# Graph layer with residual norm on one core: the last output computed by whole rows and late halves, and PSUM copies moved ahead in the first steps

## The chip, the cores and the metric

The kernel runs on one core of one Trainium2 chip. The metric is the device time of one execution in microseconds (us). The engines are named as the profile names them: PE is TensorE, DVE is VectorE, ACT is ScalarE, POOL is GpSimd, SP is the engine that issues the DMAs. Each has its own instruction queue, kept in order; they meet at semaphores only.

## What is computed

For 32 batches of x (256 x 512) and an adjacency matrix adj (256 x 256), all in float32:

```
v = x @ weight ; q = x @ wq ; k = x @ wk
alpha = max(q @ k^T, 0) * (adj != 0)
alpha = softmax(alpha, axis=1)            # over the first index n, per batch
y = x + alpha @ v
out = (y - mean(y)) / sqrt(var(y) + 1e-5) # over the 512 columns
```

## The kernel before

Two batches make a pair; there are 16 pairs, and a pair's output is four "rows" (tiles of 128 rows by 512 columns; rows 0 and 1 are the first batch, 2 and 3 the second). Every float32 operand is split into a high and a low part (`..._hi`, made by ACT, and `..._lo`, the rest, made by DVE or POOL), and each product is three matrix products, hi*hi, hi*lo, lo*hi (`add_chunk`, lines 320 to 322).

`wq @ wk^T` is folded once into one matrix g, so that a pair needs T = g*x^T, the scores S = x*T, V = x*w and the output O = P*V, with P the softmax. T and V are built by a Strassen-like scheme of seven products, P1 to P7, of 256 x 256 blocks A11, A12, A21, A22 and sums of blocks S1 to S4. P1, P6, P5, P3 accumulate in one PSUM tile `chain`, in that order, half by half (c = 0, 1). After P1, P6 and P5 ACT copies each half to the SBUF tile `parts` before the next product may be added to it: the PE waits for `t_copied` (for T) or `v_copied` (for V). P7 and P4 use `bank_y`, P2 `bank_z`; DVE adds those into `parts` (`sum_t`, line 1037; `sum_v`, line 1044), and P4 may not overwrite `bank_y` until `sum_t` has read P7 out of it (`t_summed`).

The order of each engine's work is written out by hand. The first steps (pair 0 and the second half of T for pair 1) stand apart, a loop over groups of two pairs follows, and the last pair has code of its own. In the first steps three lists matter here:

- ACT copies chain for T of pair 1 (`copy_second_t`, line 706) and, among those copies, makes the high parts of the softmax of pair 0, `split_p(0, r)` (line 771). Later come the four exponents of pair 1 (`exponent`, line 763) and the copies of chain for V of pair 1 (`copy_v`, line 711).
- DVE has, in this order, `split_p(0, 0)`, a sum, `split_p(0, 1)` to `split_p(0, 3)` (the low parts p_lo, line 1098, each after ACT's high part), `sum_t(0, A22, 0)` and `sum_t(0, A22, 1)`, then the low parts of T (line 1025) and the residual adds (line 1108). The PE's P4 halves each wait for one of those sums.
- POOL makes the block sums S3, S1, S2, S4 of pair 2 (line 1432) as soon as their input has landed.

The last pair ends with `fill_last_o`: eight halves of rows (128 x 256) on eight PSUM places, in the order rows 0, 1 (column half 0), rows 2, 3 (half 1), rows 0, 1 (half 1), rows 2, 3 (half 0). DVE adds x to each half as it comes. Rows 0 and 1 get their mean from accumulated sums and their variance from ACT's squares; rows 2 and 3 get both from DVE's bn_stats and bn_aggr. POOL raises the variances to the power -1/2, two rows at a time. ACT scales row 0, DVE rows 1, 3, 2, and SP stores each row (256 KB) as it is done, in the order 0, 1, 3, 2.

Of the kernel before, what the change touches and what calls it, by code (L numbers as in the profile page):

```python
# [5 lines left out]
ALU = mybir.AluOpType  # L6
# [5 lines left out]
P = 128  # L12
EPS = 1e-5
# [22 lines left out]
A11, A12, A21, A22 = range(4)  # L36
# [24 lines left out]
def gnn_resnorm(nc: bass.Bass, x, x_t, adj_t, w, wq_t, wk_t, out):  # L61
# [14 lines left out]
    with ExitStack() as ctx:  # L76
        def sb(name, shape, dt=F32):
            return ctx.enter_context(nc.sbuf_tensor(name, shape, dt))
# [48 lines left out]
        rstd_a = sb("rstd_a", [P, R])  # L127
        shift = sb("shift", [P, R])

        half_sum = sb("half_sum", [P, M, 2])  # L130
        half_stats = sb("half_stats", [P, M, 2, 6])
        row_stats = sb("row_stats", [P, M, 2])

# [23 lines left out]
        def w_sum(b):  # L157
# [50 lines left out]

        LAST_HALVES = [(A11, 0, 0), (A11, 1, 0), (A22, 2, 1), (A22, 3, 1),
                       (A12, 0, 1), (A12, 1, 1), (A21, 2, 0), (A21, 3, 0)]
        last_to = [o_bank[0][:, 0], o_bank[1][:, 0], o_bank[2][:, 1], bank_y[:, 0, 1],
                   bank_z[:, 1], chain[:, 0, 1], chain[:, 1, 0], bank_y[:, 1, 0]]

# [5 lines left out]
        def _(sp):  # L221
# [81 lines left out]
            for t in range(2):  # L303
                sp.wait_ge(scaled, M * t + M)
                sp.dma_start(out_rows[PAIRS - 2][:, M * t:M * t + M],
                             xn[:, 0, M * t:M * t + M]).then_inc(y_stored[0], 16)
            for k, r in enumerate((0, 1, 3, 2)):
                if r == 0:
                    sp.wait_ge(scaled, R + 1)
                else:  # L310
                    sp.wait_ge(normed, R * (PAIRS - 2) + k)
                sp.dma_start(out_rows[PAIRS - 1][:, r], xn[:, 1, r]).then_inc(y_stored[1], 16)
# [5 lines left out]
        def _(pe):  # L318
# [303 lines left out]
            def fill_last_o():  # L622

                p = PAIRS - 1

                pe.wait_ge(added, R * p)
                for (u, r, j), to in zip(LAST_HALVES, last_to):
                    g, rows = u // 2, slice(r % M * P, (r % M + 1) * P)
                    if r % M == 0:
                        pe.wait_ge(p_lo_ready, R * p + M * g + M)  # L630
                        pe.wait_ge(v_lo_ready, R * p + V_LAST[u])
                    for m in range(M):
                        t = g * M + m
# [39 lines left out]
        def _(act):  # L673
# [313 lines left out]
            split_p(0, 0, first=True)  # L987
            split_p(0, 1)
            copy_second_t(P6)
            split_p(0, 2)  # L990
            split_p(0, 3)
            copy_second_t(P5)

            act.wait_ge(s_filled, 2)
            split_second_t(A11)
# [27 lines left out]
        def _(dve):  # L1023
# [324 lines left out]
            def add_half(n):  # L1348

                _, r, j = LAST_HALVES[n]  # L1350
                half = xn[:, 1, r, j * N:(j + 1) * N]
                dve.wait_ge(half_filled, n + 1)
                if r < M:
                    nc.vector.scalar_tensor_tensor(out=half, in0=last_to[n], scalar=1.0, in1=half, op0=ALU.mult,
                                                   op1=ALU.add, accum_out=half_sum[:, r, j:j + 1]).then_inc(half_added, 1)
                else:
                    nc.vector.tensor_tensor(half, last_to[n], half, ALU.add).then_inc(half_added, 1)

            def measure_half(n, after):
                _, r, j = LAST_HALVES[n]  # L1360
                dve.wait_ge(half_added, after)
                nc.vector.bn_stats(half_stats[:, r - M, j], xn[:, 1, r, j * N:(j + 1) * N]).then_inc(half_measured, 1)

            def measure_row(r, after):
                dve.wait_ge(half_measured, after)
                nc.vector.bn_aggr(row_stats[:, r - M], half_stats[:, r - M]).then_inc(row_measured, 1)

            def mean_of(r, after):
                dve.wait_ge(half_added, after)
                nc.vector.tensor_scalar(neg_mean[:, r:r + 1], half_sum[:, r, 0:1], half_sum[:, r, 1:2], -1.0 / D,  # L1370
                                        ALU.add, ALU.mult).then_inc(mean_ready, 1)

            def normalise_last(r):

                dve.wait_ge(rstd_ready, last + (0 if r < M else 1))
                if r < M:
                    nc.vector.tensor_scalar(xn[:, 1, r], xn[:, 1, r], neg_mean[:, r:r + 1], rstd[:, r:r + 1],
                                            ALU.add, ALU.mult).then_inc(normed, 1)
                else:
                    nc.vector.tensor_scalar(xn[:, 1, r], xn[:, 1, r], row_stats[:, r - M, 0:1], rstd[:, r:r + 1],  # L1380
                                            ALU.subtract, ALU.mult).then_inc(normed, 1)

            split_p(last, 0)
            split_p(last, 1)
# [15 lines left out]
            measure_half(2, 4)  # L1400
            add_half(4)
            mean_of(0, 5)
            add_half(5)
            mean_of(1, 6)
            measure_half(3, 6)
            add_half(6)
            measure_half(6, 7)
            measure_row(2, 3)
            add_half(7)
            dve.wait_ge(squared, R * last + M)  # L1410
            nc.vector.tensor_scalar(var_eps[:, 0:M], square_sum[:, 0:M], 1.0 / D, EPS, ALU.mult, ALU.add).then_inc(var_ready, 1)
            measure_half(7, 8)
            measure_row(3, 4)
            dve.wait_ge(row_measured, M)
            nc.vector.tensor_scalar(var_eps[:, M:R], row_stats[:, :, 1], EPS, None, ALU.add).then_inc(var_ready, 1)
            normalise_last(1)
            normalise_last(3)
            normalise_last(2)

        @block.gpsimd  # L1420
        def _(pool):
# [128 lines left out]
```

## Time and profile before

| quantity | value |
|---|---|
| time, median of 3 runs | 524.33 us (523.89 to 525.05) |
| profiled execution: its time / its span | 523.82 us / 522.0 us |
| PE busy | 511.8 us, 98% of the span |
| DVE, ACT, POOL busy | 368.1 (71%), 325.8 (62%), 258.1 us (49%) |
| mean granted PE clock | 0.995 of full speed |
| DMA | 62.05 MB, mean 119 GB/s |

The span runs from the first to the last instruction of the profile; the 1.8 us that the execution takes beyond it lie outside. Busy shares are means over the span. The PE's matrix products are pipelined: a 256-column product is listed as 0.28 us long, but the next one starts 0.12 us later, and only the distance of starts tells how fast the PE goes. After a wait of the PE the first product is listed as 0.38 or 0.39 us.

### The profile page before, as it was taken

What the parts mean: (1) busy time and instruction counts of PE and PEld (TensorE: products, weight loads), DVE (VectorE), ACT (ScalarE), POOL (GpSimd) and SP (SyncE); (2) the same over time, 40 slices, a digit from 0 to 9 for tenths busy, and PEclk for the clock granted to TensorE, in tenths of its full rate; (3) what the DMA queues carried; (4) which work ended last, traced back from release to release, by engine and by line L of the source; (5) the groups of instructions that cost most, each with busy time, mean ns of one, the idle gap of its engine ahead of it and who ended that gap; (6) DMA issues with size and microseconds to landing.
All of it is one profiled execution on the core that took longest, in us unless ns stands there. A gap on an engine that the chain in (4) does not pass through costs nothing.

```text
span 522.0 us, 9934 instructions
## 1 busy us (share of the span) xinstructions
PE 511.8 (98%) x3259; PEld 466.2 (89%) x3259; DVE 368.1 (71%) x746; ACT 325.8 (62%) x747; POOL 258.1 (49%) x196
## 2 busy tenths in 40 slices
PE   8999999999999999999999999999999999999994
PEld 5889998899989998899988999889998999889994
DVE  4766846776948677586866778577684867757686
ACT  5566556476763857539574586638676385764583
POOL 0397875239635386155661486433962537710011
PEclk9999999999999999999999999999999999999998
DMA  7404241044430626025350333404351061502334
GB/s 261 182 0 161 90 155 62 21 125 152 154 115 20 213 69 241 20 52 189 109 206 21 127 138 118 166 20 161 120 200 61 20 221 60 201 1 69 133 130 192
DMA packets 30735, 62.05 MB, mean 119 GB/s; under 512 B 2048, under 2 KB 3072, under 8 KB 30720
## 3 DMA queue, kind: packets, MB, share of 16 engines
q1 hardware_dynamic: 30720, 61.87, 34.2%
q8 instruction: 7, 0.11, 0.1%
q14 instruction: 8, 0.07, 0.0%
HBM read 45.09 MB, written 16.78 MB: 119 GB/s over the span
## 4 chain that ended last, share of the span: by engine, by line
PE 94%; DVE 2%; ACT 1%; DMA 1%; issue 0%; POOLq 0%; POOL 0%; SPq 0%; DVEq 0%; ACTq 0%
PE o_bank L320 12%; PE o_bank L321 12%; PE o_bank L322 12%; PE chain L320 11%; PE chain L322 11%; PE chain L321 11%; PE bank_y L320 6%; PE bank_y L321 6%; PE bank_y L322 6%; PE bank_z L320 3%; PE bank_z L321 3%; PE bank_z L322 3%; DMA xn<-in_w 1%; PE chain L502 0%; PE chain L503 0%; ACT v_hi L755 0%
## 5 line engine op out<-in xcount | busy, mean ns | idle before, releaser
L1441 POOL TENSOR_TENSOR s_lo<-xs,s_hi 128x512 fp32r<-128x512 f32 x60 | 82.6, 1394 | 33.9 <-ACT s_hi L692 33.9
L1436 POOL TENSOR_TENSOR a_lo<-xt,a_hi 128x512 fp32r<-128x512 f32 x42 | 57.9, 1386 | 61.2 <-ACT a_hi L684 61.2
L322 PE MATMUL o_bank<-t_hi,a_lo 128*128 128x256 f32 x256 | 72.4, 283 | 0.0
L321 PE MATMUL o_bank<-t_lo,a_hi 128*128 128x256 f32 x256 | 72.4, 283 | 0.0
L320 PE MATMUL o_bank<-t_hi,a_hi 128*128 128x256 f32 x256 | 72.4, 283 | 0.0
L1432 POOL TENSOR_TENSOR xs<-xt 128x512 f32<-128x512 f32 x30 | 40.0, 1347 | 47.8 <-DMA xt<-in_x_t 30.1
L1446 POOL TENSOR_TENSOR rstd<-var_eps,minus_half 128x4 f32<-128x4 f32 x14 | 14.2, 1018 | 92.6 <-DVE var_eps L1122 92.6
L711 ACT COPY parts<-chain 128x256 f32<-128x256 f32 x90 | 33.2, 370 | 39.5 <-PE chain L322 38.4
L320 PE MATMUL chain<-w_hi,s_hi 128*128 128x256 f32 x180 | 51.0, 284 | 0.5 <-ACT parts L711 0.5
L322 PE MATMUL chain<-w_hi,s_lo 128*128 128x256 f32 x180 | 50.9, 283 | 0.0
L321 PE MATMUL chain<-w_lo,s_hi 128*128 128x256 f32 x180 | 50.9, 283 | 0.0
L321 PEld LDWEIGHTS o_bank<-t_lo,a_hi 128*128 128x128 f32 x256 | 49.1, 192 | 0.3
L320 PEld LDWEIGHTS o_bank<-t_hi,a_hi 128*128 128x128 f32 x256 | 49.1, 192 | 0.3
L322 PEld LDWEIGHTS o_bank<-t_hi,a_lo 128*128 128x128 f32 x256 | 49.1, 192 | 0.0
L320 PE MATMUL o_bank<-v_hi,p_hi 128*128 128x512 f32 (+1 forms) x126 | 48.5, 385 | 0.0
L321 PE MATMUL o_bank<-v_lo,p_hi 128*128 128x512 f32 (+1 forms) x126 | 48.5, 385 | 0.0
L1037 DVE TENSOR_TENSOR parts<-parts,bank_y 128x512 f32<-128x512 f32 (+1 forms) x32 | 20.7, 653 | 39.2 <-ACT parts L701 25.8
L322 PE MATMUL o_bank<-v_hi,p_lo 128*128 128x512 f32 (+1 forms) x126 | 48.4, 384 | 0.0
L1025 DVE TENSOR_TENSOR v_lo<-parts,v_hi 128x512 fp32r<-128x512 f32 x45 | 47.6, 1071 | 0.9 <-ACT v_hi L755 0.9
L1108 DVE SCALAR_TENSOR_TENSOR xn<-o_bank,xn 128x512 f32<-128x512 f32 x60 | 40.9, 683 | 8.4 <-PE o_bank L322 8.4
L701 ACT COPY parts<-chain 128x512 f32<-128x512 f32 x42 | 24.7, 588 | 34.6 <-PE chain L322 34.1
L783 ACT ACTIVATE c_b<-xn,neg_mean 128x512 f32<-128x512 f32 x58 | 41.9, 722 | 3.4 <-DVE neg_mean L1370 2.4
(222 smaller groups left out, 1628.9 us busy)
## 6 DMA issues: line engine op xcount, KB each, us to landing
xt<-in_x_t SPq DMA_DIRECT2D x64, 256.0 KB, 3.2
xn<-in_x SPq DMA_DIRECT2D x16, 1024.0 KB, 5.2
out<-xn SPq DMA_DIRECT2D x14, 1024.0 KB, 5.4
adj<-in_adj_t SPq DMA_DIRECT2D x16, 512.0 KB, 6.0
xn<-in_w SPq DMA_DIRECT2D x4, 256.0 KB, 4.9
xn<-in_wq_t SPq DMA_DIRECT2D x4, 256.0 KB, 5.8
parts<-in_wk_t SPq DMA_DIRECT2D x4, 256.0 KB, 5.8
out<-xn SPq DMA_DIRECT2D x2, 512.0 KB, 2.8
```

The source lines that it names most:

```text
L320: nc.tensor.matmul(dst, a[0], b[0], start=first, stop=False, skip_group_check=shared)
L321: nc.tensor.matmul(dst, a[0], b[1], start=False, stop=False, skip_group_check=shared)
L322: return nc.tensor.matmul(dst, a[1], b[0], start=False, stop=last, skip_group_check=shared)
L701: nc.scalar.copy(parts[:, PART[product], c], chain[:, c]).then_inc(t_copied, 1)
L711: nc.scalar.copy(parts[:, PART[product], c, 0], chain_v[:, c]).then_inc(v_copied, 1)
L783: nc.scalar.activation(squares, xn[:, slot, r], ACT.Square, bias=neg_mean[:, r:r + 1], accum_out=square_sum[:, r:r + 1]).then_inc(squared, 1)
L1025: return nc.vector.tensor_tensor(dst, whole, hi.bitcast(F32), ALU.subtract)
L1037: nc.vector.tensor_tensor(part, part, bank, ALU.add).then_inc(t_summed, 1)
L1108: nc.vector.scalar_tensor_tensor(out=xn[:, slot, r], in0=row.rearrange("q j n -> q (j n)"), scalar=1.0, in1=xn[:, slot, r], op0=ALU.mult, ...
L1432: nc.gpsimd.tensor_tensor(xs[:, s], a, b, op).then_inc(x_summed[slot], 1)
L1436: nc.gpsimd.tensor_tensor(a_lo[:, slot, u], xt[:, u], a_hi[:, slot, u].bitcast(F32), ALU.subtract).then_inc(a_lo_ready[slot], 1)
L1441: nc.gpsimd.tensor_tensor(s_lo[:, slot, s], xs[:, s], s_hi[:, slot, s].bitcast(F32), ALU.subtract).then_inc(s_lo_ready[slot], 1)
```

## The change

It has two parts. In the first steps ACT's list is reordered: the two copies of P5 go ahead of `split_p(0, 2)` and `split_p(0, 3)`, and the two copies of P1 for V of pair 1 go between the exponents of pair 1. At the end, rows 0 and 1 of the last output are computed whole and first, on `o_bank[0]` and `o_bank[1]`, and only rows 2 and 3 by halves; DVE uses `residual` and a mean by row, rows 2 and 3 get a variance and a power each, and they are scaled and stored in the order 2, 3.

```diff
-        LAST_HALVES = [(A11, 0, 0), (A11, 1, 0), (A22, 2, 1), (A22, 3, 1),
-                       (A12, 0, 1), (A12, 1, 1), (A21, 2, 0), (A21, 3, 0)]
+        LAST_HALVES = [(A22, 2, 1), (A22, 3, 1), (A21, 2, 0), (A21, 3, 0)]
+        last_to = [o_bank[2][:, 1], bank_y[:, 0, 1], chain[:, 0, 0], chain[:, 1, 0]]
...
-            for k, r in enumerate((0, 1, 3, 2)):
+            for k, r in enumerate((0, 1, 2, 3)):
...
                 pe.wait_ge(added, R * p)
+                pe.wait_ge(p_lo_ready, R * p + M)
+                pe.wait_ge(v_lo_ready, R * p + V_LAST[A12])
+                for r in range(M):
+                    fill_row(r, o_bank[r][:])
+                pe.wait_ge(p_lo_ready, R * p + R)
...
             copy_second_t(P6)
+            copy_second_t(P5)
             split_p(0, 2)
             split_p(0, 3)
-            copy_second_t(P5)
...
-            for r in range(R):
-                exponent(1, r)
+            exponent(1, 0)
+            exponent(1, 1)
             copy_v(1, P1, 0)
+            exponent(1, 2)
             copy_v(1, P1, 1)
+            exponent(1, 3)
...
+            def variance_of(r):
+                dve.wait_ge(row_measured, r - M + 1)
+                nc.vector.tensor_scalar(var_eps[:, r:r + 1], row_stats[:, r - M, 1:2], EPS, None, ALU.add).then_inc(var_ready, 1)
...
             sum_v(last, A21)
+            residual(last, GROUPS - 1, 1, 0)
+            mean_of(0)
             split_v(last, A21, V_LAST)
-            dve.wait_ge(xn_loaded[1], 16 * GROUPS)
-            for n in range(R):
-                add_half(n)
+            residual(last, GROUPS - 1, 1, 1)
+            mean_of(1)
...
-            for t in range(2):
-                rows = slice(M * t, M * t + M)
-                pool.wait_ge(var_ready, PAIRS + t)
+            for k, rows in enumerate((slice(0, M), slice(M, M + 1), slice(M + 1, R))):
+                pool.wait_ge(var_ready, PAIRS + k)
                 nc.gpsimd.tensor_tensor(rstd[:, rows], var_eps[:, rows], minus_half[:, rows],
                                         ALU.pow).then_inc(rstd_ready, 1)
```

What follows is how the instructions stand, engine by engine (line numbers of each kernel's own source; in the changed kernel they are shifted by 1 to 3).

ACT in the first step, before: L706 are the copies of chain, first those of P1, then P6, then P5; L771 are the high softmax parts of rows 0, 1, then 2, 3; L745 are the high parts of T.

```order
L706 COPY parts<-chain 128x256 x2
L771 ACTIVATE p_hi<-soft,inv_sum 128x256 x2
L706 COPY parts<-chain 128x256 x2
L771 ACTIVATE p_hi<-soft,inv_sum 128x256 x2
L706 COPY parts<-chain 128x256 x2
L745 CAST t_hi<-parts 128x512 x2
```

And in the changed kernel:

```order
L707 COPY parts<-chain 128x256 x2
L772 ACTIVATE p_hi<-soft,inv_sum 128x256 x2
L707 COPY parts<-chain 128x256 x4
L772 ACTIVATE p_hi<-soft,inv_sum 128x256 x2
L746 CAST t_hi<-parts 128x512 x2
```

The two copies of P5 moved ahead of the softmax parts of rows 2 and 3; nothing else did.

ACT in the second step, before: L763 are the four exponents of pair 1, L711 the copies of chain for V (P1, P6, P5, two halves each).

```order
L692 CAST s_hi<-xs 128x512 x4
L763 ACTIVATE soft,exp_sum<-soft,neg_max 128x256 x4
L711 COPY parts<-chain 128x256 x6
L684 CAST a_hi<-xt 128x512
L692 CAST s_hi<-xs 128x512
```

And in the changed kernel:

```order
L693 CAST s_hi<-xs 128x512 x4
L764 ACTIVATE soft,exp_sum<-soft,neg_max 128x256 x2
L712 COPY parts<-chain 128x256
L764 ACTIVATE soft,exp_sum<-soft,neg_max 128x256
L712 COPY parts<-chain 128x256
L764 ACTIVATE soft,exp_sum<-soft,neg_max 128x256
L712 COPY parts<-chain 128x256 x4
```

The two copies of P1 moved ahead of the third and the fourth exponent.

DVE at the end of the program, before, from the last low part of V on:

```order
L1025 TENSOR_TENSOR v_lo<-parts,v_hi 128x2x256
L1354 SCALAR_TENSOR_TENSOR xn,half_sum<-o_bank,xn 128x256 x2
L1357 TENSOR_TENSOR xn<-o_bank,xn 128x256
L1357 TENSOR_TENSOR xn<-bank_y,xn 128x256
L1362 BN_STATS half_stats<-xn 128x6
L1354 SCALAR_TENSOR_TENSOR xn,half_sum<-bank_z,xn 128x256
L1370 TENSOR_SCALAR neg_mean<-half_sum 128x1
L1354 SCALAR_TENSOR_TENSOR xn,half_sum<-chain,xn 128x256
L1370 TENSOR_SCALAR neg_mean<-half_sum 128x1
L1362 BN_STATS half_stats<-xn 128x6
L1357 TENSOR_TENSOR xn<-chain,xn 128x256
```

And in the changed kernel, from the first residual row on:

```order
L1111 SCALAR_TENSOR_TENSOR xn,y_sum<-o_bank,xn 128x512
L1370 TENSOR_SCALAR neg_mean<-y_sum 128x1
L1028 TENSOR_TENSOR v_lo<-parts,v_hi 128x2x256
L1111 SCALAR_TENSOR_TENSOR xn,y_sum<-o_bank,xn 128x512
L1370 TENSOR_SCALAR neg_mean<-y_sum 128x1
L1356 TENSOR_TENSOR xn<-o_bank,xn 128x256
L1361 BN_STATS half_stats<-xn 128x6
L1356 TENSOR_TENSOR xn<-bank_y,xn 128x256
L1398 TENSOR_SCALAR var_eps<-square_sum 128x2
L1361 BN_STATS half_stats<-xn 128x6
L1356 TENSOR_TENSOR xn<-chain,xn 128x256
```

Two whole rows with their means stand where four halves with accumulated sums stood, one of them ahead of the last low part of V, and the variance of rows 0 and 1 comes five instructions earlier in the measuring of rows 2 and 3.

## Rows read from the trace of the kernel before

**Rows 1.** Chain of waits, whole span, by engine: share of the span.
```profile
PE 94%; DVE 2%; ACT 1%; DMA 1%; issue 0%; POOLq 0%; POOL 0%; SPq 0%; DVEq 0%; ACTq 0%
```

**Rows 2.** Timeline, PE, 52 to 54.1 us: start, duration, engine, line, operation, output<-inputs, shapes.
```profile
52.10 0.28 PE L322 MATMUL chain<-s_hi,g_lo 128*128 128x256 f32 x1
52.48 0.38 PE L320 MATMUL chain<-s_hi,g_hi 128*128 128x256 f32 x1
...
54.01 0.28 PE L320 MATMUL bank_y<-a_hi,g_hi 128*128 128x256 f32 x1
```

**Rows 3.** Timeline, ACT, 50.9 to 52.8 us.
```profile
50.98 0.37 ACT L706 COPY parts<-chain 128x256 f32<-128x256 f32 x1 [0.34 <-PE chain L322]
51.25 0.91 ACT L771 ACTIVATE p_hi<-soft,inv_sum 128x256 fp32r<-128x256 f32 x2
52.06 0.73 ACT L706 COPY parts<-chain 128x256 f32<-128x256 f32 x2
```

**Rows 4.** Timeline, DVE, 51.8 to 53.4 us; in brackets idle before, and its end.
```profile
51.80 0.88 DVE L1098 SCALAR_TENSOR_TENSOR p_lo<-soft,inv_sum,p_hi 128x256 fp32r<-128x256 f32 x2 [1.36 <-ACT p_hi L771]
52.60 0.74 DVE L1037 TENSOR_TENSOR parts<-parts,bank_y 128x256 f32<-128x256 f32 x2
```

**Rows 5.** Timeline, POOL, 53 to 54.5 us.
```profile
53.23 1.30 POOL L1432 TENSOR_TENSOR xs<-xt 128x512 f32<-128x512 f32 x1 [4.28 <-DMA xt<-in_x_t]
```

**Rows 6.** Timeline, DVE and POOL, about 83.8 and about 117.5 us.
```profile
83.03 1.30 POOL L1441 TENSOR_TENSOR s_lo<-xs,s_hi 128x512 fp32r<-128x512 f32 x1 [1.62 <-ACT s_hi L692]
83.81 0.80 DVE L1098 SCALAR_TENSOR_TENSOR p_lo<-soft,inv_sum,p_hi 128x256 fp32r<-128x256 f32 x1
...
117.46 0.48 DVE L1098 SCALAR_TENSOR_TENSOR p_lo<-soft,inv_sum,p_hi 128x256 fp32r<-128x256 f32 x1
117.59 1.50 POOL L1436 TENSOR_TENSOR a_lo<-xt,a_hi 128x512 fp32r<-128x512 f32 x1 [8.55 <-ACT a_hi L684]
```

**Rows 7.** Timeline, PE, at 69.5 us: the start of P6 in the second step.
```profile
69.53 0.39 PE L320 MATMUL chain<-w_hi,s_hi 128*128 128x256 f32 x1 [0.54 <-ACT parts L711]
```

**Rows 8.** Timeline, ACT, 68.1 to 69.8 us.
```profile
68.13 0.51 ACT L763 ACTIVATE soft<-soft,neg_max 128x256 f32<-128x256 f32 x1 [1.75 <-DVE soft L1087]
...
69.13 0.62 ACT L711 COPY parts<-chain 128x256 f32<-128x256 f32 x2
```

**Rows 9.** Timeline, PE: first 512-column product of a pair, and what follows the 24.
```profile
493.48 0.40 PE L320 MATMUL o_bank<-v_hi,p_hi 128*128 128x512 f32 x1
...
498.95 0.28 PE L320 MATMUL chain<-w_hi,a_hi 128*128 128x256 f32 x1
```

**Rows 10.** Timeline, DVE, the end of the program and two rows like the new ones.
```profile
499.04 0.68 DVE L1108 SCALAR_TENSOR_TENSOR xn<-o_bank,xn 128x512 f32<-128x512 f32 x1
...
499.84 0.54 DVE L1128 TENSOR_SCALAR xn<-xn,neg_mean,rstd 128x512 f32<-128x512 f32 x1
...
508.57 0.68 DVE L1025 TENSOR_TENSOR v_lo<-chain,v_hi 128x512 fp32r<-128x512 f32 x1
...
512.74 0.43 DVE L1362 BATCH_NORM_STATS2 half_stats<-xn 128x6 f32<-128x256 f32 x1
...
514.59 0.41 DVE L1357 TENSOR_TENSOR xn<-chain,xn 128x256 f32<-128x256 f32 x1
...
516.88 0.57 DVE L1377 TENSOR_SCALAR xn<-xn,neg_mean,rstd 128x512 f32<-128x512 f32 x1
517.71 1.00 DVE L1380 TENSOR_SCALAR xn<-xn,row_stats,rstd 128x512 f32<-128x512 f32 x2 [0.26 <-POOL rstd L1521]
```

**Rows 11.** Timeline, POOL, after 516 us.
```profile
516.14 1.53 POOL L1521 TENSOR_TENSOR rstd<-var_eps,minus_half 128x2 f32<-128x2 f32 x2 [10.83 <-DVE var_eps L1411]
```

**Rows 12.** Timeline, SP's DMA issues, after 517 us.
```profile
517.62 1.82 SPq L312 DMA_DIRECT2D out<-xn  x4
```

**Rows 13.** Stretches at the end: length, busy time by engine, granted clock, DMA share, GB/s.
```profile
518.50:521.00 2.50, 0.00 (x0) 0.00 (x0) 0.21 (x1) 0.00 (x0) 0.00 (x0) 0.50 1.05 406
521.00:521.50 0.50, 0.00 (x0) 0.00 (x0) 0.00 (x0) 0.00 (x0) 0.00 (x0) 0.50 0.13 45
```

More of the change, by code:

```diff
@@ L128, in gnn_resnorm @@
         shift = sb("shift", [P, R])
-        half_sum = sb("half_sum", [P, M, 2])
         half_stats = sb("half_stats", [P, M, 2, 6])
@@ L207, in gnn_resnorm @@
             sem("half_added"), sem("half_measured"), sem("row_measured"), sem("centred"))
-        LAST_HALVES = [(A11, 0, 0), (A11, 1, 0), (A22, 2, 1), (A22, 3, 1),
-                       (A12, 0, 1), (A12, 1, 1), (A21, 2, 0), (A21, 3, 0)]
-        last_to = [o_bank[0][:, 0], o_bank[1][:, 0], o_bank[2][:, 1], bank_y[:, 0, 1],
-                   bank_z[:, 1], chain[:, 0, 1], chain[:, 1, 0], bank_y[:, 1, 0]]
+        LAST_HALVES = [(A22, 2, 1), (A22, 3, 1), (A21, 2, 0), (A21, 3, 0)]
+        last_to = [o_bank[2][:, 1], bank_y[:, 0, 1], chain[:, 0, 0], chain[:, 1, 0]]
         block = ctx.enter_context(nc.Block())
@@ L626, in fill_last_o @@
                 pe.wait_ge(added, R * p)
+                pe.wait_ge(p_lo_ready, R * p + M)
[3 more added lines that the diff above has]
+                pe.wait_ge(p_lo_ready, R * p + R)
                 for (u, r, j), to in zip(LAST_HALVES, last_to):
-                    g, rows = u // 2, slice(r % M * P, (r % M + 1) * P)
-                    if r % M == 0:
-                        pe.wait_ge(p_lo_ready, R * p + M * g + M)
+                    rows = slice(r % M * P, (r % M + 1) * P)
+                    if r == M:
                         pe.wait_ge(v_lo_ready, R * p + V_LAST[u])
                     for m in range(M):
-                        t = g * M + m
+                        t = M + m
                         last = add_chunk(to, (p_hi[:, t, rows], p_lo[:, t, rows]), (v_hi[:, t, j], v_lo[:, t, j]),
@@ L1352, in add_half @@
                 dve.wait_ge(half_filled, n + 1)
[L1353 to L1359, printed above, removed]
+                nc.vector.tensor_tensor(half, last_to[n], half, ALU.add).then_inc(half_added, 1)
@@ L1360, in measure_half, with measure_row @@
+            def measure_half(n):
                 _, r, j = LAST_HALVES[n]
-                dve.wait_ge(half_added, after)
+                dve.wait_ge(half_added, n + 1)
                 nc.vector.bn_stats(half_stats[:, r - M, j], xn[:, 1, r, j * N:(j + 1) * N]).then_inc(half_measured, 1)
-            def measure_row(r, after):
-                dve.wait_ge(half_measured, after)
+            def measure_row(r):
+                dve.wait_ge(half_measured, r + 1)
                 nc.vector.bn_aggr(row_stats[:, r - M], half_stats[:, r - M]).then_inc(row_measured, 1)
[L1368 to L1381, printed above, removed]
+            def mean_of(r):
+                dve.wait_ge(added, R * last + r + 1)
+                nc.vector.tensor_scalar_mul(neg_mean[:, r:r + 1], y_sum[:, r:r + 1], -1.0 / D).then_inc(mean_ready, 1)
@@ L1395, in _ @@
             sum_v(last, A21)
+            residual(last, GROUPS - 1, 1, 0)
+            mean_of(0)
             split_v(last, A21, V_LAST)
-            dve.wait_ge(xn_loaded[1], 16 * GROUPS)
-            for n in range(R):
-                add_half(n)
[L1400 to L1409, printed above, removed]
+            residual(last, GROUPS - 1, 1, 1)
+            mean_of(1)
+            add_half(0)
+            measure_half(0)
+            add_half(1)
             dve.wait_ge(squared, R * last + M)
             nc.vector.tensor_scalar(var_eps[:, 0:M], square_sum[:, 0:M], 1.0 / D, EPS, ALU.mult, ALU.add).then_inc(var_ready, 1)
[L1412 to L1418, printed above, removed]
+            measure_half(1)
+            add_half(2)
+            measure_half(2)
+            measure_row(2)
+            add_half(3)
+            variance_of(2)
+            measure_half(3)
+            measure_row(3)
+            variance_of(3)
+            dve.wait_ge(rstd_ready, last)
+            nc.vector.tensor_scalar(xn[:, 1, 1], xn[:, 1, 1], neg_mean[:, 1:2], rstd[:, 1:2],
+                                    ALU.add, ALU.mult).then_inc(normed, 1)
+            for r in range(M, R):
+                dve.wait_ge(rstd_ready, last + r - M + 1)
+                nc.vector.tensor_scalar(xn[:, 1, r], xn[:, 1, r], row_stats[:, r - M, 0:1], rstd[:, r:r + 1],
+                                        ALU.subtract, ALU.mult).then_inc(normed, 1)
         @block.gpsimd
```

## The prediction, made before the changed kernel had run

> **What bounds the kernel now.** The chain of waits comes first: it runs through the PE for 94% of the span [rows 1], so an edit counts only where the PE waits, or after its last product. The timeline of the PE then shows where it waits. A 256-column product normally starts 0.12 us after the one before. From 20 us on, only two distances are clearly larger, and both are waits for an ACT copy of `chain`. The first is at P3 of the first step, 0.38 us instead of 0.12 [rows 2]. The second is at P6 of the second step: an idle time of 0.54 us listed behind a product of 0.28 that normally covers 0.12, hence 0.54 + 0.16 = 0.70 [rows 7]. The first product after a wait is listed as 0.38 or 0.39 instead of 0.28 and holds up the next by 0.10 more [rows 2, 7]. From 69.53 us to the last output there is no further wait: what the first steps lose or gain arrives at the end undiminished. The end is the second place: DVE's last rows [rows 10], the powers [rows 11], and four stores that share the DMA engines [rows 12, 13].
>
> Every sum below is made against the profiled execution, 523.82 us. It lies 0.51 below the median of the runs, 524.33, and I add each difference to the median.
>
> **The copies of P5, first step: the wait that goes.** Now ACT ends the first copy of P5 at 52.06 + 0.37 = 52.43, and P3 starts at 52.48 [rows 2, 3]. P5's first half ends six products (0.72) before its second, and ACT starts about 0.32 after the start of a half's last product. The last product of the second half starts at 52.10 [rows 2], so the copies can start at 51.70 and 52.42 and end at 52.07 and 52.79. P3's halves would start at 52.22 and 52.94 unhindered: the wait goes, 0.26 + 0.10 = 0.36 us, to a few hundredths.
>
> **The same edit: the wait that comes.** `split_p(0, 2)` and `split_p(0, 3)` now stand behind the second copy, which cannot start before 52.42, where they started at 51.25 [rows 3]. Behind them on DVE stand, unmoved, p_lo of rows 2 and 3 and then the two sums of A22; P4 on the PE waits for these sums. ACT starts an activation 0.27 after a copy and 0.41 after an activation [rows 3]: high parts from 52.69 and 53.10, ready at 53.20 and 53.61. DVE follows 0.04 later [rows 3, 4]: p_lo(2) from 53.24, p_lo(3) from 53.65. A pair of p_lo takes 0.88 for two of 0.48, a distance of 0.40 [rows 4]. Undisturbed, the first sum would run from 54.05 to 54.46, and P4 would start at 54.51 and run 0.10 late, like 54.61 against 54.01 now [rows 2]: **+0.60**, with the 0.36 already in it. So even the cheapest case of this edit loses.
>
> The question is whether p_lo is undisturbed, for POOL begins its block sums of pair 2 at 53.23, when a DMA has landed [rows 5]. The rows about 83.8 and 117.5 show two instructions of this kind meeting [rows 6]. POOL started at 83.03 and ended at 84.33; the p_lo that started at 83.81 took 0.80 instead of 0.48 and ended 0.28 after POOL did. At 117.46 p_lo started first and kept its 0.48; POOL started at 117.59 and took 1.50, ending 1.15 after p_lo's end at 117.94. So the two take turns. The copy and the sums, with an operand in PSUM, I take as undisturbed: the sums at 52.60 took what they take elsewhere, and the adds that follow here read PSUM too.
>
> Now p_lo(2) would start at 53.24 and POOL's first sum at 53.23. This is a tie, and there are three outcomes:
> - *DVE first.* p_lo(2) ends at 53.72; POOL, behind it, at 53.72 + 1.15 = 54.87; p_lo(3), behind POOL, at 54.87 + 0.28 = 55.15; the first sum starts 0.08 before that and ends at 55.48; P4 at 55.53, plus 0.10. Against 54.01: **+1.62**.
> - *POOL first.* POOL ends at 54.53, p_lo(2) at 54.81, POOL's second sum at 55.96, p_lo(3) at 56.24, the sum at 56.57, P4 at 56.62 plus 0.10: **+2.71**.
> - *POOL later than 53.65*: the +0.60 above.
>
> I take the first. The instant of POOL's start hangs on a DMA, and the profiled execution is about the fastest of the runs shown, so in a median run the data land rather later than earlier against the computation. All three keep P4 as the place of the loss. Behind P4 nothing else gets late: the output row that needs DVE's first residual starts 0.10 + 2 x 0.72 + 3 x 1.37 = 5.65 us after P4 (6 x 0.228 = 1.37 a row [rows 9]), 6.1 after the first sum, and DVE's list from that sum to the residual takes about 5.4, turns with POOL included.
>
> The Trainium skill ("SBUF — State Buffer", "Who interferes with whom") says that a DVE instruction with two SBUF inputs contends with a GpSimd instruction that reads SBUF, and: "Issue order, not op shape, decides who blocks." The 0.80 and the 1.50 agree with it. Read to the letter it would give POOL's 53.23 the turn before DVE's 53.24; that is the second outcome, whose price stands above from rows alone.
>
> **The copies of P1, second step.** ACT's third exponent waits for DVE until 68.13, and the copies of P1 stand behind the fourth, at 69.13 [rows 8]. Yet P1's first half is done well before: P6 wanted to start at 68.83 (69.53 - 0.70), and two halves of 0.72 lie between, so that it ends at 67.39. In its new place the first copy finds ACT idle, in the 1.75 us before 68.13 [rows 8], and ends by about 68.0. The second follows the third exponent, about 68.6 to 69.0, and P6's second half wants it at 69.43. The fourth exponent moves back by 0.3 us, and its reader, the reciprocal, is far behind. So the wait of rows 7 goes whole: 0.70 + 0.10 = **-0.80**. Bounds: nothing gained to all of it; I take all, since ACT's idle time covers the copy.
>
> **The end.** The PE's first whole row needs the low part of V of A12, ready at 508.57 + 0.68 = 509.25 [rows 10]; it may start at 509.30, and its first product costs 0.10 extra. 24 products of 512 columns take 5.47 us [rows 9], 0.228 each: row 0's last product starts at 510.54, is 0.39 long, and DVE is there 0.10 later, 511.03. A row with its mean takes 0.80 (499.04 to 499.84) [rows 10], the low part of V between the rows 0.68 - 0.07 = 0.61. So the first half-add starts at 511.03 + 0.80 + 0.61 + 0.80 = 513.24; its products, 12 x 0.228 + 6 x 0.12 later, are done. Then come add (0.44 to its bn_stats), bn_stats (0.43 - 0.08 = 0.35), add 0.34, a variance of two columns 0.11, bn_stats 0.35 [rows 10]: the third add starts at 514.83. From there the list is the one that stands before between 514.59 and 516.88, 2.29 us [rows 10]: add, bn_stats, aggregate, add, variance, bn_stats, aggregate, variance. Row 1 is scaled from 517.12, rows 2 and 3 at distances of 0.46 (1.00 - 0.54) [rows 10], the last until 518.58. Before, it ended at 518.71, since it had to wait 0.26 for the power [rows 10, 11].
>
> That is only 0.13. The rest comes from the stores. Before, the first was issued at 517.62 [rows 12], as soon as row 0 was scaled, and 1.05 MB at 406 GB/s take 2.58 us, until about 521.06 [rows 13]; so data began to move near 518.47, 0.85 after the issue, and the queue was full until the end. Now the variance of rows 0 and 1 is ready near 514.5, its power (0.70 [rows 11]) near 515.3, and row 0 is stored from 516.1, ahead of the crowd. Three stores are left: issued from 517.69, data from 518.54, 3 x 0.65 = 1.94, until 520.48. Gain 521.06 - 520.48 = 0.58, which I round to **-0.55**. A power of one column doesn't stand in the trace; between nothing and the 0.70 of two columns [rows 11] its end, at most 517.94, is before row 3's turn at 518.04, so it costs nothing. If scaling had to take turns with it as p_lo does, 0.3 would be lost; if the last store were alone in the queue, 0.1 more gained: -0.25 to -0.65.
>
> **Sum.** +1.62 - 0.80 - 0.55 = +0.27: 524.09 in the profiled execution's terms, 524.60 in the median's. A difference of 0.2%, 1.05 us, is about what a measurement of this kernel can tell from no change; the forecast is no change.
>
> **The rivals.**
> - *POOL first* (the other side): the two p_lo of the first step each wait a whole POOL sum. For it: 53.23 is before 53.24, and the skill's rule. Against: a hundredth is less than my rounding. It decides as soon as POOL starts before DVE there. +2.71 - 0.80 - 0.55 = +1.36: 525.69, slower.
> - *POOL late, or no turns*: +0.60 - 0.80 - 0.55 = -0.75: 523.58. For it: a DMA decides. Against: it has to be 0.4 us later than in the profile.
> - *P4 doesn't wait*, as when p_lo were not ahead of the sums: -0.36 - 0.80 - 0.55 = -1.71: 522.62, faster. Against it stands DVE's list itself.
> - *The second step gains nothing* (the copy comes late for another reason) and POOL is first: +2.71 - 0.55 = +2.16: 526.49.
>
> **How the numbers follow.** Forecast 0.42, POOL first 0.32, POOL late 0.16, P4 free 0.05, no gain in the second step 0.05. The range 523.3 to 526.0 holds the first three with their bounds (the end's 0.3 either way) and leaves out the last two and some edges. The forecast's own range is 524.2 to 525.0. Slower by over 1.05 us: POOL first, less a fifth of it (if the DMA is 0.3 earlier, so is everything behind it), plus the last case: 0.31. Faster by over 1.05: P4 free and an edge of POOL late, 0.08. The rest, 0.61, is within.
>
> **What would show it.** PE: no wait at P3, but one at P4's first product of 1.9 us (DVE first), 3.0 (POOL first) or 0.9 (POOL late); none at P6 of the second step. DVE: p_lo(2) of 0.48 and p_lo(3) of about 1.5, or both over 1. The end: three stores together after 517.7 plus the shift, one alone 1.6 us before, and about 0.55 us less from the PE's last P4 to the end. It is wrong if P4 follows P3 without a wait, or if a wait appears later in the loop.

## The result: slower by 0.3%, and the profile after

Over 21 executions of each, the changed kernel takes 525.89 us (523.89 to 528.69) and the kernel before 524.64 (523.52 to 525.67): ratio 1.0030, 95% interval 1.0018 to 1.0042. I had forecast no change (+0.27 us); it is +1.3 to +1.6. The median is inside my range, but the interval leaves out "no change", which was the forecast.

The profiled execution (524.70 us, span 522.9) is one of the shorter ones, and place by place it shows nearly what was forecast. The timeline of PE at P4 of the first step, to be held against [rows 2]:

```profile
54.18 0.28 PE L319 MATMUL chain<-s_hi,g_lo 128*128 128x256 f32 x1
56.14 0.39 PE L317 MATMUL bank_y<-a_hi,g_hi 128*128 128x256 f32 x1 [1.69 <-DVE parts L1040]
```

P3 follows P5 without a wait now, and P4 waits: its first product starts 1.96 us after the one before instead of 0.12, so the wait is 1.84 (1.88 forecast for "DVE first"). The cause, on DVE and on POOL, against [rows 4] and [rows 5]:

```profile
53.87 1.89 DVE L1101 SCALAR_TENSOR_TENSOR p_lo<-soft,inv_sum,p_hi 128x256 fp32r<-128x256 f32 x2 [2.80 <-ACT p_hi L772]
55.68 0.74 DVE L1040 TENSOR_TENSOR parts<-parts,bank_y 128x256 f32<-128x256 f32 x2
```

```profile
54.21 2.69 POOL L1429 TENSOR_TENSOR xs<-xt 128x512 f32<-128x512 f32 x2 [4.62 <-DMA xt<-in_x_t]
```

The two low parts took 1.89 us together instead of 0.88, because POOL's first sum took the turn between them. In the second step P6 starts without a wait, where [rows 7] shows one:

```profile
70.70 0.28 PE L317 MATMUL bank_y<-w_hi,s_hi 128*128 128x256 f32 x1
71.06 0.28 PE L317 MATMUL chain<-w_hi,s_hi 128*128 128x256 f32 x1
```

The listing shows every third product, so 0.36 apart is full speed. At the end, on PE, DVE, POOL and SP in turn, and the stretch of the last stores, against [rows 10 to 13]:

```profile
510.84 0.47 PE L317 MATMUL o_bank<-v_hi,p_hi 128*128 128x512 f32 x1 [0.22 <-DVE v_lo L1028]
```

```profile
512.58 0.69 DVE L1111 SCALAR_TENSOR_TENSOR xn<-o_bank,xn 128x512 f32<-128x512 f32 x1 [1.16 <-PE o_bank L319]
...
518.57 0.54 DVE L1410 TENSOR_SCALAR xn<-xn,neg_mean,rstd 128x512 f32<-128x512 f32 x1
519.03 1.16 DVE L1414 TENSOR_SCALAR xn<-xn,row_stats,rstd 128x512 f32<-128x512 f32 x2
```

```profile
517.90 0.55 POOL L1517 TENSOR_TENSOR rstd<-var_eps,minus_half 128x1 f32<-128x1 f32 x1 [1.07 <-DVE var_eps L1374]
518.74 0.87 POOL L1517 TENSOR_TENSOR rstd<-var_eps,minus_half 128x1 f32<-128x1 f32 x1 [0.29 <-DVE var_eps L1374]
```

```profile
517.61 2.94 SPq L309 DMA_DIRECT2D out<-xn  x4
```

```profile
520.00:522.00 2.00, 0.00 (x0) 0.00 (x0) 0.19 (x1) 0.00 (x0) 0.00 (x0) 0.74 1.01 388
522.00:522.50 0.50, 0.00 (x0) 0.00 (x0) 0.00 (x0) 0.00 (x0) 0.00 (x0) 0.50 0.00 0
```

The first output row starts 0.50 us after the last product of P4, 0.22 of it listed as idle, and DVE, which waited 1.16 us for that row, has a full list from 512.58 on. Row 0's store is issued at 517.61, and the other three fill the DMA engines from about 520.0 to 522.0. From the first product of the last P4 (507.58 before, 509.02 after) to the end of the span, 522.01 and 522.87 to the hundredth, it is 14.43 before and 13.85 now: 0.58 less, where the sum had 0.58 and rounded it to 0.55.

The two profiled executions differ by 0.88 us, more than the +0.27 forecast, but most of that is there before the first step. One instruction of the preparation (a low part from the folding of `wq` and `wk`, not one of the softmax), which no edit touches, starts at 21.05 us before and at 21.69 after:

```profile
21.05 0.42 DVE L1235 SCALAR_TENSOR_TENSOR p_lo<-o_bank,p_hi 128x256 fp32r<-128x256 f32 x1
```

```profile
21.69 0.42 DVE L1238 SCALAR_TENSOR_TENSOR p_lo<-o_bank,p_hi 128x256 fp32r<-128x256 f32 x1
```

From there to the end of the span it is 500.96 us before and 501.18 after: +0.22, for a forecast of +0.27. In the 14 profiles of this document that start lies between 20.7 and 22.1 us, so below single executions are compared from there on.

What the profiled execution does not show is the spread. Each execution also has a mean granted clock. Ten of the 21 have 0.996 to 0.998 and a median of 524.8, where I had put the forecast; eleven have 0.991 to 0.994 and a median of 527.2 (two executions, 525.82 and 525.94, lie about where the groups meet). The kernel before has one execution below 0.995 in the 89 whose clock is recorded beside the experiments.

### The profile page after: what moved, and what is told of

It reads as the page before. It is cut to its first block, busy times and chain, and to the rows that moved or that the text cites. A ratio compares the mean times of both kernels' runs of the same rounds, so it can differ in the third digit from the quotient of the medians.

```text
span 522.9 us, 9906 instructions
## 1 busy us (share of the span) xinstructions
PE 511.4 (98%) x3247; PEld 465.8 (89%) x3247; DVE 372.1 (71%) x743; ACT 325.8 (62%) x747; POOL 255.2 (49%) x197
## 4 chain that ended last, share of the span: by engine, by line
PE 95%; DVE 2%; DMA 1%; ACT 1%; issue 1%; POOLq 0%; SPq 0%; POOL 0%; DVEq 0%; ACTq 0%
PE o_bank L317 12%; PE o_bank L318 12%; PE o_bank L319 12%; PE chain L318 11%; PE chain L319 11%; PE chain L317 11%; PE bank_y L317 6%; PE bank_y L318 6%; PE bank_y L319 6%; PE bank_z L317 3%; PE bank_z L318 3%; PE bank_z L319 3%; DMA xn<-in_w 1%; PE chain L499 0%; DVE v_lo L1028 0%
## 5 line engine op out<-in xcount | busy, mean ns | idle before, releaser
L1438 POOL TENSOR_TENSOR s_lo<-xs,s_hi 128x512 fp32r<-128x512 f32 x60 | 81.1, 1369 | 37.6 <-ACT s_hi L693 37.6
L1429 POOL TENSOR_TENSOR xs<-xt 128x512 f32<-128x512 f32 x30 | 38.6, 1298 | 47.1 <-DMA xt<-in_x_t 29.8
L317 PE MATMUL chain<-w_hi,s_hi 128*128 128x256 f32 x180 | 50.9, 283 | 0.0
L318 PE MATMUL chain<-w_lo,s_hi 128*128 128x256 f32 x180 | 50.9, 283 | 0.0
L319 PE MATMUL chain<-w_hi,s_lo 128*128 128x256 f32 x180 | 50.9, 283 | 0.0
L1131 DVE TENSOR_SCALAR xn<-xn,neg_mean,rstd 128x512 f32<-128x512 f32 x56 | 41.6, 765 | 10.1 <-POOL rstd L1443 10.1
L1111 DVE SCALAR_TENSOR_TENSOR xn<-o_bank,xn 128x512 f32<-128x512 f32 x62 | 42.3, 685 | 9.0 <-PE o_bank L319 9.0
L1040 DVE TENSOR_TENSOR parts<-parts,bank_y 128x512 f32<-128x512 f32 (+1 forms) x32 | 20.7, 653 | 39.2 <-ACT parts L702 25.8
```

What stands on the lines that cost most here:

```text
L317: nc.tensor.matmul(dst, a[0], b[0], start=first, stop=False, skip_group_check=shared)
L318: nc.tensor.matmul(dst, a[0], b[1], start=False, stop=False, skip_group_check=shared)
L319: return nc.tensor.matmul(dst, a[1], b[0], start=False, stop=last, skip_group_check=shared)
L1040: nc.vector.tensor_tensor(part, part, bank, ALU.add).then_inc(t_summed, 1)
L1111: nc.vector.scalar_tensor_tensor(out=xn[:, slot, r], in0=row.rearrange("q j n -> q (j n)"), scalar=1.0, in1=xn[:, slot, r], op0=ALU.mult, ...
L1131: nc.vector.tensor_scalar(xn[:, slot, r], xn[:, slot, r], neg_mean[:, r:r + 1], rstd[:, r:r + 1], ALU.add, ALU.mult).then_inc(normed, 1)
```

## The experiments

Theory A: the copies of P5 are the whole loss. P4 waits about 2 us with the PE idle, and an idle PE of that length makes the granted clock fall in part of the executions, which comes on top of the wait. (As first put on record it also had POOL in the first turn and a wait of 3 us in about half of the executions; no profile below shows that.) Theory B: the long executions have another cause, the new end, the copies of P1 or chance. A time below stands for the median of the experiment, beside that of the kernel before on the same chip; "low" counts executions with a mean clock under 0.995. The ratio is not the quotient of the two medians, since the median of the kernel before moves between 524.15 and 525.05 from set to set; where they differ, go by the ratio. "In the profile" is the time from the instruction at about 21 us to the end of the span, less the 500.96 of the kernel before.

| experiment | us (before) | ratio, 95% interval | wait at P4, us | in the profile, us | low |
|---|---|---|---|---|---|
| P5 put back | 522.86 (524.15) | 0.9972, 0.9962 to 0.9982 | 0.11 | -1.17 | 0 of 10 |
| P5 alone | 526.81 (524.15) | 1.0042, 1.0026 to 1.0057 | 1.90 | +3.20 | 2 of 6 |
| sums first | 524.67 (524.15) | 1.0012, 0.9996 to 1.0028 | none; 1.68 later | +0.12 | 2 of 12 |
| POOL held | 523.71 (524.15) | 0.9987, 0.9976 to 0.9999 | 0.84 | -0.77 | 0 of 12 |
| 3 fills | 525.89 (525.05) | 1.0014, 0.9998 to 1.0030 | 1.96 | +1.87 | 7 of 12 |
| 6 fills | 528.40 (525.05) | 1.0058, 1.0039 to 1.0078 | 3.13 | +1.53 | 5 of 9 |
| 9 fills | 530.03 (525.05) | 1.0104, 1.0087 to 1.0121 | 4.31 | +4.89 | 6 of 6 |
| new end alone | 523.58 (525.05) | 0.9987, 0.9975 to 1.0000 | none | -0.58 | 1 of 12 |
| extra products | 525.02 (524.54) | 1.0015, 1.0002 to 1.0028 | idle for 0.20 | +0.26 | 0 of 12 |
| changed kernel again | 526.27 (524.54) | 1.0031, 1.0015 to 1.0047 | 2.25 | +2.17 | 7 of 12 |
| one copy each | 522.95 (524.54) | 0.9972, 0.9960 to 0.9985 | 0.43 | -1.17 | 0 of 12 |
| P1 alone | 523.43 (524.54) | 0.9982, 0.9972 to 0.9992 | none | -0.81 | 0 of 12 |

The waits are those of the profiled execution: distance of two products' starts, less 0.12 us (less 0.23 for the 512-column products of the 1.68). The four profiles with a low stretch ahead of the program's end are those of P5 alone, 3 fills, 9 fills and the changed kernel again.

**P5 put back.** The changed kernel with this part undone:

```diff
             copy_second_t(P6)
-            copy_second_t(P5)
             split_p(0, 2)
             split_p(0, 3)
+            copy_second_t(P5)
```

> The changed kernel with the two copies of P5 put back behind the softmax parts of rows 2 and 3, as before; P1's copies and the new end stay. Theory A (the copies of P5 are the loss: P4 waits, and in about half the executions POOL takes the first turn, the wait is 3 us and the granted TensorE clock falls for some time): P3 waits 0.36 us again, P4 not at all, the wait at P6 of the second step stays away (-0.80), the end gains 0.55: 1.35 us less than before, about 0.3%, and no execution with a mean clock under 0.995. Theory B (the long executions come from the new end or from the copies of P1): the executions still spread by over 4 us and the median is at or above that of before.

Measured: 0.28% faster than before, 1.3 us by the medians, all executions within 1.6 us, none low. This is as A has it, and B falls as far as it names the copies of P1 and the new end: both are in this kernel. In the profile it is 1.17 less, for 1.35 forecast. Its profile shows why the old order bore the same meeting with POOL. The low parts took as long as in the changed kernel:

```profile
51.78 1.93 DVE L1101 SCALAR_TENSOR_TENSOR p_lo<-soft,inv_sum,p_hi 128x256 fp32r<-128x256 f32 x2 [1.36 <-ACT p_hi L772]
53.64 0.74 DVE L1040 TENSOR_TENSOR parts<-parts,bank_y 128x256 f32<-128x256 f32 x2
```

But they began 1.4 us earlier (51.78 against 53.87, in an execution that runs 0.65 ahead), and the first sum ended at 54.05, so that P4, at 54.10, waited 0.11 us, which with the 0.10 after it is what is missing from the forecast. The PE's other waits after 20 us were that at P3 and one of some 0.4 us ahead of the last output, which every kernel with the new end has.

**P5 alone.** The kernel before with the same edit as in the changed one and nothing else.

> The kernel before with the two copies of P5 moved ahead of the softmax parts, and nothing else. Theory A: all of the loss, since both gains are missing: at least +1.6 us where DVE has the first turn and +2.7 or more where POOL has it, with two groups of executions that differ in mean clock (0.997 against 0.993); median about 2.5 to 3.5 us above before. Theory B: +1.6 us in every execution, spread as narrow as that of before (2 us), no low clock.

Measured: 0.42% slower than before, 2.2 us, 2.7 by the medians. This part costs more than the whole change, and its profile shows a fall of the clock. Two of six executions are low, and a third, 527.31 us at 0.995, may have had a fall too. Stretches of PE: length, busy time, granted clock, DMA share, GB/s.

```profile
55.00:56.00 1.00, 0.00 (x0) 1.00 0.00 0
56.00:57.00 1.00, 1.00 (x6) 0.69 0.00 0
57.00:58.00 1.00, 1.00 (x6) 0.50 0.00 0
58.00:59.00 1.00, 1.00 (x5) 0.50 0.00 0
59.00:60.00 1.00, 1.00 (x5) 0.60 0.00 0
60.00:61.00 1.00, 1.00 (x6) 1.00 0.00 0
```

The PE waits 54 to 56, resumes at 56.00, and the clock falls from 2.4 to 1.2 GHz at 56.4, when the PE is busy again. It stays low for 3.41 us. That half the work is done meanwhile would be 1.7 us lost on top of the wait; in the profile, +3.20 less the wait of 1.90 and the 0.10 after it, plus the 0.36 that P3 gains, leaves 1.56.

**Sums first.** The changed kernel with DVE's list altered:

```diff
-            for r in range(1, R):
-                split_p(0, r)
+            split_p(0, 1)
             sum_t(0, A22, 0, one)
             sum_t(0, A22, 1, one)
+            split_p(0, 2)
+            split_p(0, 3)
```

> The changed kernel with DVE's two sums of A22 moved ahead of the low softmax parts of rows 2 and 3, so that P4 waits for copies and sums alone. Theory A: neither P3 nor P4 waits: -0.36 - 0.80 - 0.55 = -1.7 us against before, 0.33% faster, clock of every execution at least 0.995, the narrow spread of before. Theory B: the same distribution as the changed kernel, less 2 us at most, with its long executions still there.

Measured: no gain (1.0012). P3 and P4 do not wait, as forecast, but the fourth output row does, for DVE's first residual:

```profile
58.82 0.39 PE L319 MATMUL o_bank<-v_hi,p_lo 128*128 128x512 f32 x1
60.73 0.50 PE L317 MATMUL o_bank<-v_hi,p_hi 128*128 128x512 f32 x1 [1.52 <-DVE xn L1111]
```

```profile
53.08 2.33 DVE L1101 SCALAR_TENSOR_TENSOR p_lo<-soft,inv_sum,p_hi 128x256 fp32r<-128x256 f32 x2
55.33 3.48 DVE L1028 TENSOR_TENSOR t_lo<-parts,t_hi 128x512 fp32r<-128x512 f32 x2
```

Four low parts take turns with POOL's four sums, from 53.08 to 58.81, for work that takes 0.9 + 1.3 us undisturbed. The slack that I had computed behind P4 existed only because P4 was late. Both expectations missed this; on the clock the result goes with A, for with the 1.68 us of this wait there are low executions again, 2 of 12, but no profile shows one of them.

**POOL held.** The changed kernel with one line more, ahead of POOL's sums of pair 2:

```diff
+            pool.wait_ge(p_lo_ready, R)
             for s in (S3, S1, S2, S4):
```

> The changed kernel with POOL's block sums of pair 2 held back by one wait until the four low softmax parts of pair 0 are written, so that the two engines cannot meet there. Theory A: both low parts take 0.48 us, the wait at P4 is 0.9 us, +0.60 - 0.80 - 0.55 = -0.75 us against before, no long executions (clock at least 0.995). Theory B: the wait at P4 shortens by 1 us and all executions with it, but the long ones stay.

Measured: the pair of low parts takes 0.88 us, P4 waits 0.84 (0.86 forecast), no execution is low. Ratio 0.9987; -0.75 us would be 0.9986. The interval is wide (0.1 to 1.3 us faster), so the nearness is partly luck; the profile, with 0.77 less, is the better witness.

**Fills.** The kernel with POOL held, with n = 3, 6 or 9 fills on DVE to lengthen the wait alone (the lines that make `scratch` and `delayed` are left out):

```diff
+            dve.wait_ge(p_lo_ready, R)
+            for n in range(3):
+                dve.wait_ge(delayed, n)
+                nc.vector.memset(scratch[:], 0.0).then_inc(delayed, 1)
             sum_t(0, A22, 0, one)
```

> The kernel with POOL held back (wait at P4 of 0.9 us, 12 executions at 523.7 median, none under a mean clock of 0.996), and on DVE three fills of a scratch tile of 256 columns, each after the one before, between the low softmax parts and the sums that P4 waits for. Each should take about 0.3 to 0.4 us, so the wait becomes about 1.9 us. Theory A (the wait itself, at this length, makes the granted clock fall in some executions, for some 3.4 us, which costs 1.7): +1.0 in every execution, and a part of them, some three in ten, 1.7 us above the others with a mean clock of 0.991 to 0.994. Theory B (the fall of the clock comes from POOL's and DVE's turns or from chance, not from the wait): +1.0, one group, no low clock.

> As the kernel with three fills, with six: the wait at P4 about 2.9 us. Theory A: +2.0 against the kernel with POOL held, and more executions in the long group than with three fills, over half. Theory B: +2.0, one group.

> As the kernel with three fills, with nine: the wait at P4 about 3.9 us. Theory A: nearly every execution has the low clock, +3.0 + 1.7 = +4.7 against the kernel with POOL held, about 528.4 us. Theory B: +3.0, 526.7 us, one group.

Measured: low executions 0 of 12 at 0.84 us (no fills), 7 of 12 at 1.96, 5 of 9 at 3.13, 6 of 6 at 4.31. DVE and POOL do not meet here ahead of P4, so their turns do not bring the fall. (The kernel with no fills ran on another chip; there the low ones were 0 of 28 of the kernel before, here 1 of 26.) With three fills the groups have medians of 524.2 and 526.7. The profile with three fills has a fall and lies 2.64 above that of the kernel with POOL held, for a wait 1.12 longer: 1.5 for the fall. With nine, the profile shows the low clock for 6.83 us, from 2.0 us before the PE resumes; it lies 5.66 above, for a wait 3.47 longer, so the 4.87 us of low clock that are left cost 2.2. By the ratios it lies 6.1 above. The profile with six fills has no fall, after a wait of 3.13, and lies 2.30 above, for a wait 2.29 longer. That the share did not rise from three to six fills is within what 12 and 9 executions can show. Two executions with six fills, 528.40 and 528.75 at 0.996, are not explained.

**New end alone.** The kernel before with the part of the diff that concerns the last output.

> The kernel before with the new end alone (whole rows 0 and 1 first, rows 2 and 3 by halves with a power each). By my sum 0.55 us less than before (0.1%), between 0.25 and 0.65: in the profile 13.1 us from the first product of the last P4 to the end of the span before, 12.5 now. The rival, that the end gains nothing since the last store waits as before for row 3's scaling, would give 0 to -0.15.

Measured: ratio 0.9987 (0.9975 to 1.0000), 0.7 us with some 0.6 either way, and one low execution without a wait at P4, as the kernel before has one; the sum of 0.55 fits, and the rival's 0 to 0.15 is just inside the interval. The profiles decide: 0.58 here, and 13.85 or 13.86 us from the last P4 to the end also with P5 put back, against 14.42 with P1 alone, which has the old end. The 13.1 and 12.5 us of the expectation come out when counted from the last product of that P4 instead of the first: 13.11 before, 12.53 here.

**Extra products, and the changed kernel again on the same chip.**

```diff
                 t_half(P3, 1, one)
+                pe.wait_ge(v_lo_ready, 4)
+                for _ in range(14):
+                    nc.tensor.matmul(o_bank[0][:, 0], s_hi[:, 1, 0, 0, 0:P], s_hi[:, 1, 0, 0], start=True, stop=True)
                 pe.wait_ge(t_summed, 3)
```

> The changed kernel in which the PE, instead of idling before P4 of the first step, first runs 14 more products of 256 columns (about 1.7 us) into a PSUM bank that the output rows later overwrite; the wait at P4 has the same cause and end. Theory A (an idle PE makes the granted clock fall, and that is what the long executions lose): no execution below a mean clock of 0.995, the upper group is gone, and the median is about 1 to 1.5 us under that of the changed kernel on the same chip (some 524.5), though more work is done. Theory B (the length of the delay, not the idleness, makes the long executions; or the two groups are another effect of the turns with POOL): the two groups stay as they are.

> The changed kernel once more, word for word, as the measure on the same chip for the kernel with the extra products. Both theories: a median near 525.9, about half of the executions with a mean clock of 0.991 to 0.994, and those some 2.5 us longer than the others.

Measured: 525.02 against 526.27 us, 0 of 12 low against 7 of 12. If the extra products changed nothing, chance would split the low executions so unevenly in about 0.5% of cases. PE in the kernel with the extra products, L444, which cover the wait nearly to its end:

```profile
54.38 1.84 PE L444 MATMUL o_bank<-s_hi 128*128 128x256 f32 x14
56.26 0.39 PE L317 MATMUL bank_y<-a_hi,g_hi 128*128 128x256 f32 x1
```

And the changed kernel again, in an execution with the fall, PE's products and stretches:

```profile
53.21 0.28 PE L319 MATMUL chain<-s_hi,g_lo 128*128 128x256 f32 x1
55.58 0.39 PE L317 MATMUL bank_y<-a_hi,g_hi 128*128 128x256 f32 x1 [2.09 <-DVE parts L1040]
```

```profile
55.00:56.00 1.00, 0.42 (x3) 1.00 0.00 0
56.00:57.00 1.00, 1.00 (x9) 0.78 0.00 0
57.00:58.00 1.00, 1.00 (x6) 0.50 0.00 0
58.00:59.00 1.00, 1.00 (x4) 0.50 0.00 0
59.00:60.00 1.00, 1.00 (x4) 0.52 0.00 0
60.00:61.00 1.00, 1.00 (x6) 1.00 0.00 0
```

P4 starts 2.00 us after P3's last product with the extra products, 1.96 and 2.37 in the two profiles of the changed kernel; what differs is whether the PE was idle. This is the test that tells A from B. The price of a fall can be read here as well: the second profile of the changed kernel lies 2.17 - 0.22 = 1.95 us above the first, for a wait 0.41 longer, so 1.54 for the fall. In this execution POOL came first, by 0.68 us:

```profile
52.90 2.30 DVE L1101 SCALAR_TENSOR_TENSOR p_lo<-soft,inv_sum,p_hi 128x256 fp32r<-128x256 f32 x2 [2.81 <-ACT p_hi L772]
```

```profile
52.22 2.69 POOL L1429 TENSOR_TENSOR xs<-xt 128x512 f32<-128x512 f32 x2 [3.60 <-DMA xt<-in_x_t]
```

POOL's sum ended at 53.5, the first low part 0.3 after it, and the wait at P4 was 2.25 us, between my two cases.

**One copy each.** The kernel with P5 put back, but each copy where its half is ready (the change to `copy_second_t`, which now takes the halves, is left out):

```diff
             split_p(0, 2)
+            copy_second_t(P5, (0,))
             split_p(0, 3)
-            copy_second_t(P5)
+            copy_second_t(P5, (1,))
```

> The changed kernel with each copy of P5 in the place where its half is ready: high part of row 2, first copy, high part of row 3, second copy. ACT should start the first copy at 51.70, the high part of row 3 at 51.97 and the second copy at 52.42; P3's wait goes (-0.36 against the copies put back), and the sums of A22 are done by 53.35 if POOL is not in the turn before the low part of row 3, so P4 does not wait. Then -1.7 us against before. If POOL's first sum starts before 52.5, as in the profile with the copies put back (52.15), the low part of row 3 waits for it and P4 0.6 us: -1.1. Rival: no gain over the copies put back, because POOL usually is first.

Measured: 0.9972, the same as with both put back. POOL was first (52.30 against 52.72), the second low part took 1.20, and P4 waited 0.43: the rival's case, and in the profile, too, both are 1.17 under before. Both are the fastest versions, about 0.28% under the kernel before and 0.6% under the changed one.

**P1 alone.** The kernel before with the copies of P1 between the exponents.

> The kernel before with the two copies of P1 between the exponents of the second step, and nothing else. My sum: the wait at P6 of the second step goes, -0.80 us (0.15%), and no other wait appears. The rival, that the later exponents give it back further on, would show a new distance over 0.24 us between products after 70 us and a gain near 0.

Measured: 0.9982, 0.94 us (0.4 to 1.5), and 0.81 in the profile; 0.80 forecast. No PE wait is left in the profile after P3.

## Why the prediction was wrong, by its steps

- **The wait that goes (-0.36)** and **P1's copies (-0.80)**: right. Neither wait is in the profile after, and P1 alone gave 0.81 in its profile.
- **The wait that comes**: the place, the cause and the price of one execution were right. The wait at P4 was 1.84 us where 1.88 was forecast for "DVE first", and 0.84 where 0.86 was forecast without POOL. The first profile has +0.22 in all; with the measured gains of 0.81 and 0.58 set aside, +1.61 is left for this edit, +1.62 in the sum.
- **"This is a tie"** was wrong. I read one start of POOL, 53.23, as if it could move by tenths. Against the first of the two low parts POOL started 0.34 later in the profile after, 0.15 later with the extra products, 0.68 earlier in the changed kernel again and 1.03 earlier with P5 alone. The spread is about as wide as one of its sums, so the outcomes lie between the two cases: waits of 1.84, 1.90, 2.25. None of 3.0 is in a profile; the other executions have none. That the first profile came so near the forecast for "DVE first" is luck in this respect.
- **The step that failed** is the one that the sum took for granted: that a wait of the PE costs its length and 0.10 for the product after it. The sum had nothing for the clock. In every kernel with a wait of 1.68 us or more part or all of the executions are low, and a fall of 3.41 us to 1.2 GHz cost a further 1.5 to 1.6 us in three profiles. By their mean clock, 11 of 21 and 7 of 12 executions of the changed kernel have a fall. The groups differ by 2.4 us (524.8 and 527.2) in the first set and 1.5 in the second. Most of that is in the mean clocks too: the eight executions of the first set at 0.993 or 0.994 have a median of 526.4, 1.6 above the others, and the three at 0.991 have 528.6, 3.8 above. The profiles with one fall of 3.41 us and the new end have 0.993 and 0.994, the one with 6.83 us has 0.990, so those three probably had the longer fall; no profile shows it for the changed kernel. My estimate from the profiles, eight falls at 1.5 and three at twice that over 21 executions, is +1.0; added to my +0.27, it is close to the +1.25 of the medians. No rival had the term: "POOL first" has nearly the right size, 525.7, but by a wait of 3.0 us that no profile shows, and that the median lay in my range is luck.
- **The end (-0.55)**: 0.58 in the profiles. Two bounds of it did come about and cost nothing there: the power of one column took 0.55, and the second, beside DVE's scaling, 0.87; row 3 was scaled until 520.19, 0.17 us later than the sum has it from the start of P4. The DMA engines were full with the other stores by then (393 GB/s from 520.0 to 520.5).
- **"Behind P4 nothing else gets late"** was right for the changed kernel and wrong as a rule: with P4 on time, the fourth output row waits 1.68 us for the same list on DVE.

## What to carry to other kernels

When an edit takes a short wait from the PE, write down what is queued behind the instruction that moved: here 0.36 us were bought with a wait five times as long, because two instructions moved 1.4 us back into a stretch in which another engine works. Price a wait of the PE by the clock too: with a wait of 0.84 us none of 12 executions was low here, with waits of about 2 us about half were. And look at more than one execution: the profiled one had no fall and lay 1.2 us below the median. To compare two profiles, start both at an instruction that the edit doesn't touch, behind the first loads: from there the small terms of this change (0.58, 0.81, 0.77) came out to a few hundredths, while the medians left half a microsecond open.

## What the runs showed of the hardware

- The granted clock can fall after the PE has resumed: with P5 alone 0.4 us after, with three fills 0.6, in the changed kernel again 1.0 us after the end of the wait; with nine fills it fell 2.0 us before that end. It came back after 3.41 us, with nine fills after 6.83. It didn't fall in the changed kernel with a wait of 1.84 us, nor with six fills and one of 3.13. What decides between them, no run here shows.
- Low executions are there without a long wait as well, but rarely: 1 of 89 of the kernel before, 1 of 12 with the new end alone.
- At the end of the program it falls too: 2.3 us after the last product before, 4.3 us in the changed kernel, with nothing left for it to slow. The mean clock counts this stretch, 1.2 to 5.1 us of it in the 14 profiles, so 0.995 is not a sharp border between executions with and without a fall.
- The one-column power took 0.55 us, two columns 0.70, four 1.02.
- The kernel before has two groups of its own, near 523.9 and 525.3 us, at the same mean clock. No run here looked for their cause; a median of few executions of it moves by that much. The start at about 21 us varies by as much, 1.4 us, from profile to profile; whether the groups are that, isn't shown.
